# Cross-attention and routed FFN in one kernel: shared-weight splitting moved two row blocks ahead, two matmul chunks moved ahead of the last output products

## The chip, the cores and the metric

The kernel runs on one NeuronCore of one Trainium2 chip. The metric is the device time of one execution in microseconds. Before the change three runs took 1860.28, 1855.86 and 1855.59 us: median 1855.86 us.

## The reference

`x` has 4096 rows (4 x 1024) of 512 values. The block computes cross-attention against 64 keys per batch, and then a feed-forward network with one shared net and one of two routed experts:

```python
x = x + xattn(_layernorm(x), ctx, masks, Wq, Wk, Wv, Wo, bo)     # 16 heads of 64, softmax over 64 keys
z = _layernorm(x)
top1   = argmax(softmax(z @ gate_w.T))                            # one of 2 experts per row
expert = relu(z @ w1[top1] + b1[top1]) @ w2[top1] + b2[...]       # hidden size 2048
shared = relu(z @ sw1 + sb1) @ sw2 + sb2                          # hidden size 2048
x = x + expert + shared
```

## The kernel before

**Accuracy.** Operands of the large products are fp16 pairs, a high part and a low part, and each product is three matmuls (high x high, high x low, low x high). So the weights `sw1` and `sw2` of the shared net, which arrive as fp32, must be scaled and split into two fp16 halves before they can be used.

**Three stages.** Attention (until about 480 us) goes over 32 row blocks of 128 rows. The shared net goes over 16 tiles of 256 rows. The routed experts go over 17 tiles. All five engines run their own instruction streams, and semaphores tie them together. Between attention and the shared net TensorE has no barrier: it goes from the last `attend` straight to `shared_tensor`.

**A step of attention.** Every engine walks over steps t = N*g + u (N = 4), one for each row block, and in each step works on blocks at different distances: `step(eng, g, u, d, fn)` runs `fn` for block t + d. What an engine does in a step is in a fixed order:

- TensorE (`attend_tensor`): `t_p`(t) transposes the probabilities of block t into PSUM `pP` (L474, 8 matmuls); `sim`(t+2) makes the scores of block t+2 (L464, 24 matmuls of 512 columns); `attend`(t) makes the output product of block t (L485, 24 matmuls of 512 columns). `attend`(t) waits for `lo_p`(t). In steps 30 and 31 there is no `sim` left.
- ScalarE (`attend_scalar`): `hi_p`(t) (L540), `exp`(t+1) (L573), `scale_w`(t+2) (L567 and L569), `normal2`(t-1) (L554, L555), `normal`(t+4) (L546, L547).
- VectorE (`attend_vector`): `residual`(t-1) (L759), `lo_p`(t) (L703), sums, masks and statistics.
- GpSimd (`attend_gpsimd`): `lo_x`(t+3) (L344), two deviations, `norm`(t+1) (L659), `sub`(t+2) (L654), `low_w`(t+2) (L672), `lo_z`(t-1) (L668).
- SyncE (`attend_sync`) issues the DMAs of the step: `turn_x`(t+3), `load_x`, `load_m`, `load_r`(t+1), `store_x1`(t-2), `load_w`(t+3) (L393), `store_w`(t+1) (L401 and L402), `store_z`(t-2) (L416).

**Splitting of the shared weights.** Since `sw1` and `sw2` together are 32 pieces of 128 x 512, one piece is split in each step: `load_w` brings it into `sw`, `scale_w` writes the high half `swh` and scales `sw` in place, `low_w` writes the low half `swl`, `store_w` writes both halves to memory (`s1_split`, `s2_split`). All three buffers are double, by the piece's parity, and so every part waits for the piece two before it:

```python
def load_w(e, g, u):
    wait_apart(e, S["swl"], count(g, u) - 2)
def store_w(e, g, u):
    wait_apart(e, S["swl"], count(g, u))
def scale_w(e, g, u):
    e.wait_ge(S["sw_in", u % 2], dma_count2(g, u))
    e.wait_ge(S["sw_out", u % 2], 2 * dma_count2(g, u) - 32)
```

The last line is for both stores of piece r-2 to have landed before `scale_w`(r) writes `swh`. `count(g, u)` is the block's number plus one.

**Into the shared net.** The buffer `zT` of the shared net lies in the same room as `sw`, `swh` and `swl`, and the weight set `wA` in that of the folded attention weights, which `sim` reads. So `load_next` (SyncE, step 30) waits for all 32 pieces to be stored, issues two DMA transposes for `zT` (L1063), waits for `sim`(31), and loads the first quarter of the shared weights (`load_w1_w2(0)`: two DMAs at L1165, two at L1168, 512 KB each). The second quarter follows in step 32, the other two in `shared_sync`. Tile 0 of the shared net is 16 chunks: `first`(j) (L1081, 12 matmuls of 256 columns) makes 128 hidden columns, ScalarE and VectorE turn them into `hf`, `hh`, `hl`, and `second`(j) (L1093) follows two chunks later. `first`(j) waits for `hh` of chunk j-2.

## Time and profile before

| | before |
|---|---|
| time, median of 3 runs | 1855.86 us |
| profiled execution, its own time | 1857.37 us |
| span of the profiled execution | 1855.7 us |
| TensorE matmul busy | 1816.3 us (98%) |
| ScalarE busy | 820.8 us (44%) |
| VectorE busy | 797.8 us (43%) |
| GpSimd busy | 509.2 us (27%) |
| mean granted TensorE clock | 0.996 |

The profile is of one execution; its span runs from the first to the last instruction, and its own time is 1.7 us more. A busy share near 100% says that TensorE is the engine to look at, and then what counts is the few places where it stood still or ran slowly. In the rows further down, a row of a timeline gives the start in us, the length, the engine, the line, the operation with its output and input, and how many; in brackets stands how long the engine had been idle before and what released it. SPq is SyncE's queue of DMA issues, PEld the weight loads of TensorE.

### The profile page before, as it was taken

To read this page: it belongs to the slowest core of one execution; us is meant where nothing else is said; L and a number is where in the kernel's file an instruction comes from. 1 tells how busy PE (TensorE), PEld (TensorE's weight loads), DVE (VectorE), ACT (ScalarE), POOL (GpSimd) and SP (SyncE) were. 2 spreads that over 40 slices of the span, in tenths; PEclk is the share of its full clock that TensorE was granted. 3 is DMA by queue.
4 is the path that set the end of the run, shared out by engine and by line. 5 is a ranking of instruction groups with operands and counts; after the bars stand their busy time and mean duration, and the time that the engine had idled before them with its cause. 6 is when DMAs were issued, how large, how long until landed. Compare 5 with 4: busy or idle time off the path is not lost.

```text
span 1855.7 us, 33404 instructions
## 1 busy us (share of the span) xinstructions
PE 1816.3 (98%) x11516; PEld 1145.4 (62%) x11517; DVE 797.8 (43%) x1651; ACT 820.8 (44%) x1441; POOL 509.2 (27%) x475
## 2 busy tenths in 40 slices
PE   8989999999999999999999999999999999999997
PEld 6334444544566666666666666666666666666664
DVE  6987778777344333343433333222222222222222
ACT  4655555555333333334444444333333343333333
POOL 2047777777101111211100011312211221221210
PEclk9999999999999999999999999999999999999999
DMA  9246555655932332323444493921111122121100
GB/s 330 86 95 158 161 164 165 177 165 137 296 130 81 99 95 82 100 80 125 126 156 138 142 332 105 264 55 46 47 46 45 39 57 54 51 61 47 46 24 15
DMA packets 225955, 214.44 MB, mean 116 GB/s; under 512 B 126635, under 2 KB 168140, under 8 KB 225484
## 3 DMA queue, kind: packets, MB, share of 16 engines
q1 hardware_dynamic: 216924, 188.09, 34.4%
q0 software_dynamic: 8944, 25.19, 4.4%
q8 instruction: 54, 0.88, 0.2%
q14 instruction: 33, 0.27, 0.1%
HBM read 129.57 MB, written 59.02 MB: 102 GB/s over the span
## 4 chain that ended last, share of the span: by engine, by line
PE 88%; DVE 5%; POOL 2%; issue 2%; DMA 1%; ACT 1%; SPq 0%; POOLq 0%; DVEq 0%; ACTq 0%
PE pS L1081 36%; PE pP L1093 18%; PE pG L1093 9%; PE pO L1093 9%; PE pO L485 7%; PE banks_a L464 4%; PE pS L464 3%; DVE seen L799 2%; DVE room_w L819 1%; PE pP L474 1%; POOL room_b L659 1%; POOL room_b L654 1%; DMA e_split<-room_b 0%; POOL room_a L344 0%; PE banks_a L507 0%
## 5 line engine op out<-in xcount | busy, mean ns | idle before, releaser
L1081 PE MATMUL pS<-room_a,room_w 128*128 128x256 f16 (+1 forms) x6336 | 765.0, 271 | 1.5 <-issue 1.1
L1081 PEld LDWEIGHTS pS<-room_a,room_w 128*128 (+1 forms) x6336 | 611.2, 98 | 182.1 <-issue 10.2
L1112 DVE TENSOR_TENSOR room_a<-room_a 128x256 f16<-128x256 f32 (+1 forms) x528 | 237.6, 450 | 906.3 <-ACT room_a L1106 894.9
L1093 PE MATMUL pP<-room_w,room_a 128*128 (+1 forms) x1584 | 383.5, 379 | 0.1
L1104 ACT ACTIVATE room_a<-pS,room_b,sc 128x256 f32<-128x256 f32 (+1 forms) x272 | 151.7, 558 | 420.4 <-PE pS L1081 395.7
L1104 ACT ACTIVATE room_a<-pS,b1s,sc 128x256 f32<-128x256 f32 x256 | 144.2, 563 | 370.0 <-PE pS L1081 365.2
L1093 PEld LDWEIGHTS pP<-room_w,room_a 128*128 128x128 f16 x1584 | 154.8, 98 | 132.2 <-issue 0.7
L1093 PE MATMUL pG<-room_w,room_a 128*128 128x512 f16 (+1 forms) x768 | 207.6, 379 | 0.5 <-DVE room_a L1112 0.5
L1093 PE MATMUL pO<-room_w,room_a 128*128 128x512 f16 (+1 forms) x768 | 207.5, 379 | 0.0
L1128 POOL TENSOR_TENSOR room_a<-room_a,room_b 128x512 f32<-128x512 f32 x32 | 42.7, 1354 | 516.6 <-DVE room_a L1119 516.6
L485 PE MATMUL pO<-room_w,room_b 128*128 (+1 forms) x768 | 174.4, 384 | 7.6 <-DVE room_b L703 7.5
L1106 ACT ACTIVATE room_a<-pS,room_b,sc 128x256 f16<-128x256 f32 (+1 forms) x272 | 149.5, 550 | 0.0
L1106 ACT ACTIVATE room_a<-pS,b1s,sc 128x256 f16<-128x256 f32 x256 | 142.2, 556 | 0.0
L485 PEld LDWEIGHTS pO<-room_w,room_b 128*128 128x128 f16 x768 | 75.7, 99 | 101.3 <-DVE room_b L703 8.7
L1093 PEld LDWEIGHTS pO<-room_w,room_a 128*128 128x128 f16 x768 | 75.2, 98 | 90.6
L1508 POOL DMA_INDIRECT rows_room<-z_split,room_b x33 | 33.8, 1024 | 256.3 <-DVE room_b L1499 235.6
L1093 PEld LDWEIGHTS pG<-room_w,room_a 128*128 128x128 f16 x768 | 75.1, 98 | 40.6 <-DVE room_a L1112 0.8
L554 ACT ACTIVATE room_b<-room_b,shift,rs 128x512 f32<-128x512 f32 x32 | 26.1, 815 | 153.6 <-DVE shift L738 153.6
L464 PE MATMUL banks_a<-room_w,room_a 128*128 (+1 forms) x384 | 85.5, 379 | 3.2 <-DMA room_a<-room_a 1.6
L464 PE MATMUL pS<-room_w,room_a 128*128 (+1 forms) x384 | 85.5, 379 | 0.0
L1559 POOL DMA_INDIRECT out<-room_a,room_b x33 | 33.6, 1018 | 181.5 <-DVE room_a L1119 176.7
L1553 POOL TENSOR_TENSOR room_a<-room_a,room_b 128x512 f32<-128x512 f32 x33 | 44.0, 1350 | 113.8 <-DVE room_b L1641 113.8
(180 smaller groups left out, 1540.8 us busy)
## 6 DMA issues: line engine op xcount, KB each, us to landing
room_b<-in_w SPq DMA_DIRECT2D x64, 512.0 KB, 5.0
e_split<-room_b SPq DMA_DIRECT2D x64, 256.0 KB
room_w<-e_split SPq DMA_DIRECT2D x8, 2048.0 KB
rows_room<-in_x SPq DMA_DIRECT2D x32, 256.0 KB, 3.1
room_a<-in_sw SPq DMA_DIRECT2D x32, 256.0 KB, 4.2
room_b<-in_x SPq DMA_DIRECT2D x32, 256.0 KB, 3.8
s_split<-room_a SPq DMA_DIRECT2D x64, 128.0 KB, 3.7
x_scratch<-room_b SPq DMA_DIRECT2D x32, 256.0 KB, 4.0
```

The lines of the kernel that those rows point to most:

```text
L464: mm = e.matmul(pS[u % 2][:, h * 512:(h + 1) * 512], xT[:, u % 2, c, :], f[:, k, bass.ds(b, 1), h * 512:(h + 1) * 512], start=(n == 0), st ...
L485: mm = e.matmul(pO[:, :], pt[:, q, :], f[:, bass.ds(b, 1), q, :], start=(n == 0), stop=(n == 3 * PAIRS - 1))
L799: dve.tensor_reduce(dst, t, AX.X, ALU.max, apply_absolute_value=True).then_inc(done, 1)
L1081: mm = q.matmul(self.pH[j % 2][:, 0:rows], w[:, k, j * P:(j + 1) * P], zt[:, u, k, 0:rows], start=(n == 0), stop=(n == 3 * KC - 1))
L1093: mm = q.matmul(self.pY[u][r][:, :], h[:, j % self.HR, r * P:(r + 1) * P], w[:, j, :], start=(j == 0 and n == 0), stop=(j == HC - 1 and n ...
L1104: q.activation(self.hf[:, j % self.HR, 0:rows], self.pH[j % 2][:, 0:rows], ACT.Relu, bias=b, scale=self.a1)
L1106: q.activation(self.hh[:, j % self.HR, 0:rows], self.pH[j % 2][:, 0:rows], ACT.Relu, bias=b, scale=self.a1).then_inc(self.S["hh"], 1)
L1112: q.tensor_tensor(self.hl[:, j % self.HR, 0:rows], self.hf[:, j % self.HR, 0:rows], self.hh[:, j % self.HR, 0:rows], ALU.subtract).then_in ...
L1128: v = q.tensor_tensor(net.ob[:, u, r, :], net.ob[:, u, r, :], brow[:, :], ALU.add)
L1508: q.indirect_dma_start(dst[:, u, r, :], None, src, bass.IndirectOffsetOnAxis(ap=rows[:, u, r:r + 1], axis=0), bounds_check=ROWS - 1, oob_i ...
L1553: v = q.tensor_tensor(net.rb[:, u, r, :], net.rb[:, u, r, :], sel[:, u, :], ALU.add)
L1559: q.indirect_dma_start(out, bass.IndirectOffsetOnAxis(ap=io[:, u, r:r + 1], axis=0), net.ob[:, u, r, :], None, bounds_check=ROWS - 1, oob_ ...
```

## The change

`weight_steps(g, u, d)` gives the distances at which a part of the splitting runs in a step. In steps 0 to 3 it is d as before. In step 4 it is d and d+1, in step 5 it is d+1 and d+2, and from step 6 on it is d+2. So steps 4 and 5 handle two pieces each, and from then on every part works two pieces further ahead. SyncE, ScalarE and GpSimd use it for `load_w`, `store_w`, `scale_w` and `low_w`.

On SyncE `load_next`, now only the waits and the two transposes, moves from step 30 to step 28; the first quarter of the shared weights is loaded in step 29 and the second in step 30. On TensorE `first_chunk` puts chunks 0 and 1 of tile 0 between `t_p` and `attend` of steps 30 and 31, and `shared_tensor` leaves them out.

```diff
--- before.py
+++ after.py
@@ -339,6 +339,13 @@
 
                     return isinstance(g, int) and 0 <= N * g + u + d <= 1
 
+                def weight_steps(g, u, d):
+
+                    t = N * g + u if isinstance(g, int) else SUB
+                    if t < N:
+                        return (d,)
+                    return (d, d + 1) if t == N else (d + 1, d + 2) if t == N + 1 else (d + 2,)
+
                 def lo_x(e, g, u):
                     e.wait_ge(S["xn"], count(g, u))
                     e.tensor_tensor(xs[:, u % 2, DM:2 * DM], xnf[:, u % 2, :], xs[:, u % 2, 0:DM], ALU.subtract).then_inc(S["xl"], 1)
@@ -425,13 +432,19 @@
                                 sp.wait_ge(f_done, NF)
                             step(sp, g, u, 1, load_r)
                             step(sp, g, u, -2, store_x1)
-                            step(sp, g, u, 3, load_w)
-                            step(sp, g, u, 1, store_w)
+                            for d in weight_steps(g, u, 3):
+                                step(sp, g, u, d, load_w)
+                            for d in weight_steps(g, u, 1):
+                                step(sp, g, u, d, store_w)
                             step(sp, g, u, -2, store_z)
-                            if isinstance(g, int) and N * g + u == SUB - 2:
+                            if N * g + u == SUB - 4:
                                 load_next()
-                            if isinstance(g, int) and g == SUB // N and u == 0:
+                            if N * g + u == SUB - 3:
+                                sp.wait_ge(S["sim"], SUB)
+                                load_w1_w2(0)
+                            if N * g + u == SUB - 2:
                                 load_w1_w2(1)
+                            if g == SUB // N and u == 0:
                                 return
                     def load_next():
 
@@ -440,9 +453,6 @@
                             sp.wait_ge(S["z_out", u], 32)
                         for t in range(2):
                             snet.transpose(sp, t, z_d[t * TOK:(t + 1) * TOK, :])
-                        sp.wait_ge(S["sim"], SUB)
-                        load_w1_w2(0)
-
                     def load_w1_w2(q):
                         load_quarter(sp, wA, s1_d, s2_d, q, 1, first_in[f"w1_in{q}"])
                         load_quarter(sp, wA, s1_d, s2_d, q, 2, first_in[f"w2_in{q}"])
@@ -453,6 +463,12 @@
                     return last_block
 
                 def attend_tensor(pe):
+                    def first_chunk(e, j):
+                        if j == 0:
+                            e.wait_ge(S["smask"], SUB)
+                            e.wait_ge(first_in["w1_in0"], 32)
+                        snet.first(e, 0, 0, j, wA, 16)
+
                     def sim(e, g, u):
                         e.wait_ge(S["xT_in", u % 2], dma_count2(g, u))
                         at_least(e, S["smask"], count(g, u) - 2)
@@ -494,6 +510,8 @@
                             step(pe, g, u, 0, t_p)
                             if not first_tile(g, u, 0):
                                 step(pe, g, u, 2, sim)
+                            if isinstance(g, int) and SUB - 2 <= N * g + u < SUB:
+                                first_chunk(pe, N * g + u - SUB + 2)
                             step(pe, g, u, 0, attend)
 
                     pe.wait_ge(in_ctx, 16)
@@ -602,7 +620,8 @@
                             step(act, g, u, 0, hi_p)
                             step(act, g, u, 1, exp)
                             if not first_tile(g, u, 2):
-                                step(act, g, u, 2, scale_w)
+                                for d in weight_steps(g, u, 2):
+                                    step(act, g, u, d, scale_w)
                             step(act, g, u, -1, normal2)
                             if not early(g, u, 4):
                                 step(act, g, u, 4, normal)
@@ -693,7 +712,8 @@
                                 step(pool, g, u, 4, lo_x)
                             step(pool, g, u, 1, norm)
                             step(pool, g, u, 2, sub)
-                            step(pool, g, u, 2, low_w)
+                            for d in weight_steps(g, u, 2):
+                                step(pool, g, u, d, low_w)
                             step(pool, g, u, -1, lo_z)
                     groups(pool, SUB // N, body, peel_last=1)
 
@@ -1308,8 +1328,11 @@
 
     def shared_tensor(pe):
         def first(q, g, u, j):
-            if isinstance(g, int) and g == 0 and u == 0 and j % (HC // Q) == 0:
-                q.wait_ge(S[f"w1_in{j * Q // HC}"], 32)
+            if isinstance(g, int) and g == 0 and u == 0:
+                if j < 2:
+                    return
+                if j % (HC // Q) == 0:
+                    q.wait_ge(S[f"w1_in{j * Q // HC}"], 32)
             net.first(q, g, u, j, wA, 16)
 
         def second(q, g, u, j):
```

**SyncE in step 4, where the doubled steps begin.** A row is a line of the kernel, the operation with output and input, and in brackets the semaphores it waits for. `in_sw1` and `in_sw2` are the two weights; odd pieces are of `sw2`. Before, from `store_x1`(2):

```order
L412 DMA x1_scratch<-room_b 128x512 [waits a_x1]
L393 DMA room_a<-in_sw2 128x512 [waits a_swl]
L401 DMA s2_split<-room_a 128x512 [waits a_swl]
L402 DMA s2_split<-room_a 128x512
L416 DMA z_split<-room_b 128x1024 [waits a_z]
```

In the change:

```order
L419 DMA x1_scratch<-room_b 128x512 [waits a_x1]
L400 DMA room_a<-in_sw2 128x512 [waits a_swl]
L400 DMA room_a<-in_sw1 128x512 [waits a_swl]
L408 DMA s2_split<-room_a 128x512 [waits a_swl]
L409 DMA s2_split<-room_a 128x512
L408 DMA s1_split<-room_a 128x512 [waits a_swl]
L409 DMA s1_split<-room_a 128x512
L423 DMA z_split<-room_b 128x1024 [waits a_z]
```

The loads of pieces 7 and 8 now stand ahead of the stores of pieces 5 and 6, and those ahead of `store_z`(2). Step 5 has the same form with loads 9 and 10 and stores 7 and 8.

**ScalarE in step 4**, from `hi_p`(4) to `hi_p`(5). Before:

```order
L540 ACTIVATE room_b<-pP 128x1024 [waits a_att,a_pT]
L573 ACTIVATE room_b<-room_b 128x1024 [waits a_sub]
L567 ACTIVATE room_a<-room_a,sc 128x512 [waits a_sw_out0,a_swl,a_sw_in0]
L569 ACTIVATE room_a<-room_a,sc 128x512 [waits a_swh]
L554 ACTIVATE room_b<-room_b,shift2,rs2 128x512 [waits a_z_out1,a_rs2]
L555 ACTIVATE room_b<-room_b,shift2,rs2 128x512
L546 ACTIVATE room_a<-rows_room,shift1,rs1 128x512 [waits a_xT_in0,a_rs]
L547 ACTIVATE room_a<-rows_room,shift1,rs1 128x512
L540 ACTIVATE room_b<-pP 128x1024 [waits a_att,a_pT]
```

In the change:

```order
L558 ACTIVATE room_b<-pP 128x1024 [waits a_att,a_pT]
L591 ACTIVATE room_b<-room_b 128x1024 [waits a_sub]
L585 ACTIVATE room_a<-room_a,sc 128x512 [waits a_sw_out0,a_swl,a_sw_in0]
L587 ACTIVATE room_a<-room_a,sc 128x512 [waits a_swh]
L585 ACTIVATE room_a<-room_a,sc 128x512 [waits a_sw_out1,a_swl,a_sw_in1]
L587 ACTIVATE room_a<-room_a,sc 128x512 [waits a_swh]
L572 ACTIVATE room_b<-room_b,shift2,rs2 128x512 [waits a_z_out1,a_rs2]
L573 ACTIVATE room_b<-room_b,shift2,rs2 128x512
L564 ACTIVATE room_a<-rows_room,shift1,rs1 128x512 [waits a_xT_in0,a_rs]
L565 ACTIVATE room_a<-rows_room,shift1,rs1 128x512
L558 ACTIVATE room_b<-pP 128x1024 [waits a_att,a_pT]
```

`scale_w`(7), with its wait for the stores of piece 5 (`a_sw_out1`), now stands between `scale_w`(6) and `normal2`(3), and so ahead of `hi_p`(5).

**TensorE in steps 30 and 31.** Before:

```order
L474 MATMUL pP<-ident,room_b 128x128 x7
L485 MATMUL pO<-room_w,room_b 128x512 [waits a_x1,a_pTl]
L485 MATMUL pO<-room_w,room_b 128x512 x23
L474 MATMUL pP<-ident,room_b 128x128 [waits a_pTl,a_prob]
L474 MATMUL pP<-ident,room_b 128x128 x7
L485 MATMUL pO<-room_w,room_b 128x512 [waits a_x1,a_pTl]
L485 MATMUL pO<-room_w,room_b 128x512 x23
L1081 MATMUL pS<-room_a,room_w 128x256 [waits s_z_in0,s_w1_in0]
```

In the change:

```order
L490 MATMUL pP<-ident,room_b 128x128 x7
L1101 MATMUL pS<-room_a,room_w 128x256 [waits s_z_in0,s_w1_in0,a_smask]
L1101 MATMUL pS<-room_a,room_w 128x256 x11
L501 MATMUL pO<-room_w,room_b 128x512 [waits a_x1,a_pTl]
L501 MATMUL pO<-room_w,room_b 128x512 x23
L490 MATMUL pP<-ident,room_b 128x128 [waits a_pTl,a_prob]
L490 MATMUL pP<-ident,room_b 128x128 x7
L1101 MATMUL pS<-room_a,room_w 128x256 x12
L501 MATMUL pO<-room_w,room_b 128x512 [waits a_x1,a_pTl]
L501 MATMUL pO<-room_w,room_b 128x512 x23
L1101 MATMUL pS<-room_a,room_w 128x256 [waits s_hh]
```

The two chunks of 12 matmuls moved from behind the last output product into the places between transpose and product; the first one brings the wait for `zT` and the first quarter of `w1` with it.

## Rows read from the trace of the kernel before

**Rows 1.** The page: the chain that ended last, by engine

```profile
PE 88%; DVE 5%; POOL 2%; issue 2%; DMA 1%; ACT 1%; SPq 0%; POOLq 0%; DVEq 0%; ACTq 0%
```

**Rows 2.** Waits of TensorE over the whole span: in total, times, longest

```profile
PE pO L485 <- DVE room_b L703: 7.5, 4, 2.4
```

**Rows 3.** Timeline of the end of attention, steps 29 to 31, and tile 0

```profile
454.85 5.34 PE L485 MATMUL pO<-room_w,room_b 128*128 128x512 f16 x24
...
460.03 1.04 PE L474 MATMUL pP<-ident,room_b 128*128 128x128 f32 x8
...
462.16 1.22 DVE L703 SCALAR_TENSOR_TENSOR room_b<-pP,room_b 128x1024 f16<-128x1024 f32 x1 [0.45 <-ACT room_b L540]
...
463.44 7.04 PE L485 MATMUL pO<-room_w,room_b 128*128 128x512 f16 x24 [2.37 <-DVE room_b L703]
...
465.82 0.15 PEld L485 LDWEIGHTS pO<-room_w,room_b 128*128 128x128 f16 x1 [0.28 <-issue]
...
473.73 7.04 PE L485 MATMUL pO<-room_w,room_b 128*128 128x512 f16 x24 [2.37 <-DVE room_b L703]
...
480.61 4.09 PE L1081 MATMUL pS<-room_a,room_w 128*128 128x256 f16 x36
```

**Rows 4.** Busy time by stretch; the column after POOL is the granted TensorE clock

```profile
464.90:467.90 3.00, 3.00 (x8) 1.06 (x7) 1.28 (x6) 1.52 (x2) 2.66 (x3) 0.50 0.50 140
...
474.80:478.20 3.40, 3.40 (x9) 1.22 (x8) 1.20 (x7) 1.52 (x2) 1.15 (x1) 0.50 0.99 302
```

**Rows 5.** The chain that ended last, in order of time: one chunk

```profile
512.41 1.31 PE pS L1081 x12
```

**Rows 6.** Timeline of TensorE in step 0 of attention

```profile
118.39 5.35 PE L464 MATMUL banks_a<-room_w,room_a 128*128 128x512 f16 x24 [1.63 <-DMA room_a<-room_a]
...
127.00 5.35 PE L485 MATMUL pO<-room_w,room_b 128*128 128x512 f16 x24 [2.38 <-DVE room_b L703]
```

**Rows 7.** Timeline of steps 4 to 6

```profile
169.89 0.71 ACT L567 ACTIVATE room_a<-room_a,sc 128x512 f16<-128x512 f32 x1
...
170.63 0.72 ACT L569 ACTIVATE room_a<-room_a,sc 128x512 f32<-128x512 f32 x1
...
174.17 0.42 SPq L393 DMA_DIRECT2D room_a<-in_sw  x1
...
175.88 0.81 ACT L554 ACTIVATE room_b<-room_b,shift,rs 128x512 f32<-128x512 f32 x1 [4.53 <-DVE shift L738]
...
177.73 1.16 POOL L672 TENSOR_TENSOR room_a<-room_a 128x512 f16<-128x512 f32 x1
...
178.72 1.00 ACT L540 ACTIVATE room_b<-pP 128x1024 f16<-128x1024 f32 x1
...
182.43 1.21 DVE L703 SCALAR_TENSOR_TENSOR room_b<-pP,room_b 128x1024 f16<-128x1024 f32 x1
...
183.70 5.35 PE L485 MATMUL pO<-room_w,room_b 128*128 128x512 f16 x24 [0.36 <-DVE room_b L703]
...
190.98 1.16 POOL L672 TENSOR_TENSOR room_a<-room_a 128x512 f16<-128x512 f32 x1
...
195.32 5.34 PE L485 MATMUL pO<-room_w,room_b 128*128 128x512 f16 x24
```

**Rows 8.** The line L402, 160 to 450 us: its DMAs, from issue to landing

```profile
DMA to landing us min/median/max: 3.1/3.9/4.6
```

**Rows 9.** Timeline of SyncE's queue at the end of attention

```profile
445.27 0.54 SPq L401 DMA_DIRECT2D s_split<-room_a  x1
...
465.51 4.34 SPq L1063 DMA_TRANSPOSE room_a<-z_split  x2
...
470.19 0.93 SPq L1165 DMA_DIRECT2D room_w<-s_split  x2
```

**Rows 10.** DMAs issued at 470.0 to 471.1 us: size, us to landing

```profile
room_w<-s_split SPq DMA_DIRECT2D x2, 512.0 KB, 5.5
```

**Rows 11.** The line L1165 over the span: from issue to landing

```profile
DMA to landing us min/median/max: 5.0/8.0/9.0
```

## The prediction, made before the changed kernel was run

> **What bounds the kernel now.** I read the page's chain first, then who TensorE waited for, then the timeline at the two places that the change touches, then the granted clock there. The chain that ended last is TensorE for 88% [rows 1], so only its idle or slow stretches can be won, and every new one is lost in full. TensorE's costliest wait inside attention is that of `attend` for VectorE's `lo_p`: 7.5 us in four waits [rows 2]. Two of them, 2.37 us each, stand in steps 30 and 31. In a usual step `sim`(t+2) runs between `t_p` and `attend` and covers the way over `hi_p` and `lo_p`; in the last two steps nothing covers it. And after these two waits the 24 matmuls of `attend` take 7.04 us, where from 454.85 to 460.03 they took 5.18 [rows 3]. The weight loads show the pace there: 0.15 us and then 0.28 idle, 0.43 us a matmul [rows 3], and the granted clock is 0.50, the lower level of 1.2 GHz [rows 4]. So each of the two places holds 2.37 us of standstill and 7.04 - 5.18 = 1.86 us of slow clock.
>
> **The change at the end of attention.** Two chunks move from behind the last `attend` into these gaps. A chunk lasts 1.31 us at the full clock [rows 5]. It fits into 2.37 us, and `hi_p` and `lo_p` go on beside it unchanged, so 2 x 1.31 = **2.6 us** are won. What is left of each gap is 1.06 us. After 1.63 us of standstill in step 0 the next 24 matmuls took 5.35 us, and after 2.38 us also 5.35; the same idle of 2.37 us in steps 30 and 31 gave 7.04 [rows 3, 6]. So 2.4 us sometimes brings the lower clock and 1.6 us did not. I take it that 1.06 us does not, and book another 2 x 1.86 = **3.7 us**. Together **-6.3 us**; the bounds are -2.6 (clock falls all the same) and -6.3.
>
> The Trainium skill, "TensorE: Matmul & The Clock Gate", Part 1 (the HAM clock gate), says that the number of slow matmuls varies from run to run of one kernel, since the point where the clock changes does not follow the program. The trace agrees in that gaps of 2.37 and 2.38 us ended differently [rows 3, 6]. By that rule any value between the bounds is possible, and its price is the third rival below.
>
> Does the weight arrive in time? Chunk 0 can start when `t_p`(30) is done, at 463.44 - 2.37 = 461.07, and costs nothing up to 463.44 - 1.31 = 462.13 [rows 3]. SyncE stores the last piece in step 28, now 31 instead of 29, at about 445.3 to 445.9 [rows 9]; it lands 3.5 us later (the value is argued below), the two transposes take 4.34 us to issue [rows 9], and `load_r`, `store_x1` and `store_z` of step 29 some 1.4 us (three issues of 0.42 to 0.54 [rows 7, 9]): about 455. `sim`(31) ends at 454.85 [rows 3], so it does not hold it further. The two w1 loads are out by 455.9 (0.93 us for two [rows 9]), and landed 5.5 us after issue when the same load stood behind the same transposes [rows 10]: 461.0 to 461.4. That is in time, by less than 1 us. With 9.0 us to landing [rows 11] it would be 464.5. The stores of steps 28 to 30 and the second quarter have more room; chunk 2 needs `hh`(0) from chunk 0, and the whole `attend`(31), 5.18 us, lies between chunks 1 and 2 to cover it. After that the shared net runs as before.
>
> **The change in steps 4 and 5.** Here it adds waits. No work is added over the kernel, 32 pieces stay 32 pieces, but two are handled in each of these steps, and the order within SyncE and ScalarE makes a chain. `load_w`(8) waits for `low_w`(6), which GpSimd does late in step 4. Behind it on SyncE stand the stores of pieces 5 and 6 and `store_z`(2). `scale_w`(7) on ScalarE waits for the store of piece 5 to land. Behind `scale_w`(7) stand `normal2`(3), `normal`(8) and `hi_p`(5), and `hi_p`(5) releases `lo_p`(5), for which `attend`(5) waits. Worked out from the timeline of steps 4 to 6 [rows 7]:
>
> - `low_w`(6) ends at 177.73 + 1.16 = 178.9. Before, nothing on SyncE waited for it in that step: `load_w`(7) went out at 174.17 and the stores behind it.
> - The load and the high half go ahead of the low half, about 0.5 us each with what lies between: the low half is issued at 179.9.
> - Landing: 3.1 to 4.6 us, median 3.9, for this store [rows 8]. Those have up to a load, a transpose and two stores ahead; this one has one load and one store ahead and an otherwise empty queue. I take 3.5: 183.4.
> - `scale_w`(7) takes 1.46 us (169.89 to 171.35): 184.9.
> - `normal2` and `normal` take 178.72 - 175.88 = 2.84 us: `hi_p`(5) starts at 187.7 instead of 178.72.
> - `hi_p` 1.0, `lo_p` and release 463.44 - 462.16 = 1.3 [rows 3]: `attend`(5) starts at 190.0 instead of 183.70, **+6.3 us**.
>
> ScalarE's 4.53 us of idle before `normal2`(3) [rows 7] cannot hide it, since `scale_w`(7) would have to be done at 175.9 and gets its release at 183.4. Slack there is none: TensorE already waited 0.36 us for `lo_p`(5).
>
> Step 5 does it again: `load_w`(10) waits for `low_w`(8), the store of piece 7 stands behind it, `scale_w`(9) waits for that store, `hi_p`(6) stands behind `scale_w`(9). The place of `low_w`(8) in step 5 is that of `low_w`(7) before, whose end is 192.14 - 182.43 = 9.7 us after `lo_p`(5) began. The latter now begins at 188.7: `low_w`(8) ends at 198.4, the store has landed at 202.9, `hi_p`(6) starts at 207.2, `attend`(6) at 209.5 instead of 195.32: **+14.2 us** in all. From step 6 on each part again takes one piece, at the same distances between its partners as before; TensorE then has `sim` as cover and stands no more.
>
> TensorE stood idle some 6 us before each of these `attend`s, more than the 2.37 us that brought the lower clock twice. The slow stretch in `attend`(5) is hidden in the second standstill; that in `attend`(6) is not: **+1.9**, the price of rows 3. Early part: 14.2 + 1.9 = **+16.1 us**. Bounds: landing at 3.1 us in both chains and no slow clock gives 13.4, landing at 4.6 gives 18.3.
>
> The Trainium skill, "DMA: Bandwidth & Descriptors", section on latency and other measured facts, gives about 2 us as the fixed cost of a DMA. With 2.0 in place of 3.5 the estimate of the early part would be 3.0 less and the sum +6.8, 1862.7 us. No DMA of that line in the trace landed in under 3.1 us [rows 8], so I keep 3.5.
>
> **Sum.** +16.1 - 6.3 = **+9.8 us**. The profiled execution took 1857.37 us, so it would be 1867.2; that execution lies 1.5 above the median of the three runs. Against the median of 1855.86 the forecast is **1865.7 us**.
>
> **Rivals.**
> - *The doubled steps cost nothing.* The place is `scale_w`(7) in step 4. It costs nothing if its release comes by 175.88 - 1.46 = 174.4, into ScalarE's idle 4.53 us. Then only the gain is left: 1855.86 - 6.3 = 1849.5 us. For it: the total work is the same and ScalarE is 44% busy. Against it: in SyncE's order `load_w`(8) stands ahead of the store of piece 5, and it can't pass before 178.9. Chance 0.06.
> - *Only one of the two chains holds.* If in step 5 ScalarE's wait falls within a delay that step 4 has made for everybody, the early part is 6.3 + 1.9 = 8.2, the sum +1.9, 1857.8 us. For it: step 5 begins late on all engines. Against it: `low_w`(8) moves with `lo_p`(5), so the chain moves as a whole. Chance 0.13.
> - *The clock falls at the end all the same.* The gain is 2.6 and the sum 16.1 - 2.6 = +13.5: 1869.4 us. For it: TensorE is idle for 1.06 us behind a short chunk. Against it: 1.63 us did nothing in step 0. Chance 0.15.
> - *The first quarter comes late.* Landed at 464.5, chunk 0 ends at 465.8, 2.4 us after the old start of `attend`(30), and its clock stays low. Of the end are left +2.4 - 1.31 for chunk 0 and -1.31 - 1.86 for chunk 1, in sum -2.1: +14.0, 1869.9 us. This is also the case in which the change does not do what it says. For it: a margin under 1 us and loads of this line that took up to 9.0 us [rows 11]. Against it: 5.5 us for the comparable one [rows 10]. Chance 0.08.
>
> **How the numbers follow.** The forecast has 0.58. A measurement of this kernel can tell about 0.3%, 5.6 us, from no change. Forecast (its own bounds 1863.0 to 1868.0), third and fourth rival lie above 1861.4: slower 0.81. The second rival is the same, 0.13; the first is faster, 0.06. The range goes from 1857.5, which takes in the single chain, to 1871.5, the upper bound of the early part with the lower one of the gain (18.3 - 2.6 = +15.7).
>
> **What would show it.** In the changed profile, TensorE idle about 6 us before the `attend`s of steps 5 and 6, released by `lo_p`; ScalarE idle before the second `scale_w` of steps 4 and 5, released by a DMA `s_split<-room_a`; at the end one chunk of 12 matmuls in each gap, some 1 us idle behind it, and 5.2 instead of 7.04 us for the last two `attend`s. I am wrong if steps 5 and 6 start within 2 us of their old times, or if chunk 0 waits for a DMA.

## The result, and the profile after

The changed kernel took 1867.61 us (median of 6 runs, 1865.87 to 1871.35) against 1857.38 us for the kernel before (6 runs, 1855.59 to 1860.28): 10.2 us more, ratio 1.0059 with a 95% interval of 1.0045 to 1.0072. The forecast was +9.8 us. Of all executions timed below one is slow and stands in no ratio: one of the kernel with the unread matmuls, 2622.37 us at a mean granted clock of 0.685.

The page of the changed kernel: span, and the chain that ended last by engine.

```profile
span 1865.7 us, 33409 instructions
...
PE 91%; DVE 5%; DMA 1%; ACT 1%; issue 1%; POOL 1%; SPq 0%; ACTq 0%; POOLq 0%; DVEq 0%
```

The work is the same and TensorE still bounds the kernel, as in [rows 1]. What grew is its wait for `lo_p`, from 7.5 us [rows 2] to 14.2. Waits of TensorE, whole span: in total, times, longest.

```profile
PE pO L501 <- DVE room_b L723: 14.2, 4, 5.9
```

The timeline of the changed kernel in steps 4 to 7. The columns are those of [rows 7], which hold the same steps before; the first `attend` below is that of step 4.

```profile
175.62 5.34 PE L501 MATMUL pO<-room_w,room_b 128*128 128x512 f16 x24
...
180.38 1.16 POOL L691 TENSOR_TENSOR room_a<-room_a 128x512 f16<-128x512 f32 x1
...
182.42 0.43 SPq L409 DMA_DIRECT2D s_split<-room_a  x1
...
185.33 0.72 ACT L585 ACTIVATE room_a<-room_a,sc 128x512 f16<-128x512 f32 x1 [11.35 <-DMA s_split<-room_a]
...
186.71 0.80 ACT L572 ACTIVATE room_b<-room_b,shift,rs 128x512 f32<-128x512 f32 x1
186.72 0.75 DVE L779 SCALAR_TENSOR_TENSOR room_b<-pO,sc,room_b 128x512 f32<-128x512 f32 x1 [7.00 <-DMA z_split<-room_b]
...
189.53 1.00 ACT L558 ACTIVATE room_b<-pP 128x1024 f16<-128x1024 f32 x1
...
190.56 1.22 DVE L723 SCALAR_TENSOR_TENSOR room_b<-pP,room_b 128x1024 f16<-128x1024 f32 x1 [2.36 <-ACT room_b L558]
...
191.84 6.71 PE L501 MATMUL pO<-room_w,room_b 128*128 128x512 f16 x24 [4.82 <-DVE room_b L723]
...
199.12 1.16 POOL L691 TENSOR_TENSOR room_a<-room_a 128x512 f16<-128x512 f32 x1
...
201.15 0.43 SPq L409 DMA_DIRECT2D s_split<-room_a  x1
...
204.00 0.72 ACT L585 ACTIVATE room_a<-room_a,sc 128x512 f16<-128x512 f32 x1 [11.16 <-DMA s_split<-room_a]
...
210.52 7.61 PE L501 MATMUL pO<-room_w,room_b 128*128 128x512 f16 x24 [5.91 <-DVE room_b L723]
...
224.01 5.34 PE L501 MATMUL pO<-room_w,room_b 128*128 128x512 f16 x24
```

The reader is to follow one chain: `low_w`(6) ends at 181.54, SyncE issues the low half of piece 5 at 182.42, `scale_w`(7) starts when it has landed, after 11.35 us in which ScalarE did nothing, and everything down to `attend`(5) stands behind it. From 199.12 the same again. From the start of `attend`(4) to that of `attend`(7) are 48.39 us, before 206.55 - 171.94 = 34.61: **+13.8 us**.

The end of attention in the changed kernel, steps 29 to 31 and the first chunk of `shared_tensor` (compare [rows 3]):

```profile
471.15 5.34 PE L501 MATMUL pO<-room_w,room_b 128*128 128x512 f16 x24
...
478.33 1.47 PE L1101 MATMUL pS<-room_a,room_w 128*128 128x256 f16 x12 [0.97 <-issue]
479.74 5.35 PE L501 MATMUL pO<-room_w,room_b 128*128 128x512 f16 x24
...
485.81 1.47 PE L1101 MATMUL pS<-room_a,room_w 128*128 128x256 f16 x12
488.34 5.35 PE L501 MATMUL pO<-room_w,room_b 128*128 128x512 f16 x24 [1.07 <-DVE room_b L723]
493.53 1.47 PE L1101 MATMUL pS<-room_a,room_w 128*128 128x256 f16 x12
```

Both chunks run in the gaps and both `attend`s take 5.35 us. From `attend`(29) to chunk 2 are 22.38 us; before, chunk 2 came two chunks after 480.61, 483.22 - 454.85 = 28.37: **-6.0 us** in this pair of executions.

**The whole difference of the two spans, 10.0 us:** +3.7 before step 4 (`attend`(4) starts at 175.62 against 171.94), +13.8 in steps 4 to 6, -1.2 over steps 7 to 28 (247.14 against 248.30 us; 22 full steps of 11.23 are 247.1), -6.0 at the end, and -0.3 in the 1370 us that follow. The 1.2 us are small waits of the kernel before that are gone: five output products between steps 9 and 14 came 0.1 to 0.3 us late each, and TensorE's transposes waited four times for GpSimd's `norm` in steps 7 to 28; in the changed kernel each of these steps is 11.23 or 11.24 us long. The 3.7 us stand before anything that was changed. The first matmuls of the kernel before:

```profile
7.68 5.10 PE L507 MATMUL banks_a<-room_b,room_a 128*128 128x256 f32 x16 [7.68 <-DMA room_a<-in_wkT]
```

The same matmuls and the output product of step 0 of the changed kernel:

```profile
8.54 6.25 PE L525 MATMUL banks_a<-room_b,room_a 128*128 128x256 f32 x16 [8.54 <-DMA room_a<-in_wkT]
...
128.99 7.04 PE L501 MATMUL pO<-room_w,room_b 128*128 128x512 f16 x24 [2.38 <-DVE room_b L723]
```

The changed kernel began 0.9 us later behind an input DMA, its first 16 matmuls took 1.2 us longer, and the output product 1.7 us longer; before, the latter took 5.35 us behind the same idle [rows 6]. The product's slow matmuls stand at a lower granted clock (0.63 in the mean of 128.99 to 132.00 us). For the first 16 the profile shows a granted clock of 1.00 in both kernels, so that they were slower is shown, and why is not. So one pair of profiles can't settle a question of 3 us here, and the experiments below were timed in five rounds each.

### The profile page after: what moved, and what is told of

It is laid out like the page before. It is cut to its first block, busy times and chain, and to the rows that moved or that the text cites. A ratio compares the mean times of both kernels' runs of the same rounds, so it can differ in the third digit from the quotient of the medians.

```text
span 1865.7 us, 33409 instructions
## 1 busy us (share of the span) xinstructions
PE 1818.7 (97%) x11516; PEld 1146.8 (61%) x11517; DVE 797.3 (43%) x1651; ACT 822.5 (44%) x1441; POOL 510.3 (27%) x475
## 4 chain that ended last, share of the span: by engine, by line
PE 91%; DVE 5%; DMA 1%; ACT 1%; issue 1%; POOL 1%; SPq 0%; ACTq 0%; POOLq 0%; DVEq 0%
PE pS L1101 36%; PE pP L1113 18%; PE pG L1113 9%; PE pO L1113 9%; PE pO L501 9%; PE banks_a L480 4%; PE pS L480 4%; DVE seen L819 2%; DVE room_w L839 1%; PE pP L490 1%; PE banks_a L525 0%; DMA e_split<-room_b 0%; DMA room_a<-in_wkT 0%; PE banks_a L539 0%; DMA s_split<-room_a 0%
## 5 line engine op out<-in xcount | busy, mean ns | idle before, releaser
L501 PE MATMUL pO<-room_w,room_b 128*128 (+1 forms) x768 | 176.3, 387 | 14.2 <-DVE room_b L723 14.2
```

What stands on the lines that cost most here:

```text
L501: mm = e.matmul(pO[:, :], pt[:, q, :], f[:, bass.ds(b, 1), q, :], start=(n == 0), stop=(n == 3 * PAIRS - 1))
```

## The experiments

"Before" is the kernel before, run on the same chip between the others (medians 1857.1 to 1857.7 us). Timed kernels have 5 to 12 runs; they were timed in three groups on three chips (the first four versions below; early weights, one doubled step, w1 first and unread matmuls; transposes behind the stores and the changed kernel again), so versions of different groups are best compared by their distances to before; the spread of single runs of one kernel is about 2 us (standard deviation). Ratios are to before, with 95% intervals.

### The doubled steps alone

```diff
-                            if N * g + u == SUB - 4:
+                            if isinstance(g, int) and N * g + u == SUB - 2:
                                 load_next()
-                            if N * g + u == SUB - 3:
                                 sp.wait_ge(S["sim"], SUB)
                                 load_w1_w2(0)
...
-                                first_chunk(pe, N * g + u - SUB + 2)
```

> The changed kernel with its end of attention put back (second-step splitting stays doubled in steps 4 and 5, the first quarter of the weights is loaded in step 30, no chunk is moved). Theory (two chains over load_w, the store and scale_w in steps 4 and 5): the whole early cost without the gain, 14 to 16 us slower than before, about 1872 us, with TensorE idle 5 to 6 us before the output products of steps 5 and 6 and 7.0 us for each of the last two. Rival (the changed kernel is slow because its profiled execution lost 3.7 us before step 4 by chance, and the early part costs little): 4 to 8 us slower than before.

Measured: 1871.67 us, 14.2 above before, ratio 1.0074 (1.0061 to 1.0087). Its output products of steps 4 to 7:

```profile
174.12 5.34 PE L499 MATMUL pO<-room_w,room_b 128*128 128x512 f16 x24
...
190.19 8.01 PE L499 MATMUL pO<-room_w,room_b 128*128 128x512 f16 x24 [4.68 <-DVE room_b L719]
...
208.84 7.04 PE L499 MATMUL pO<-room_w,room_b 128*128 128x512 f16 x24 [4.58 <-DVE room_b L719]
...
221.77 5.34 PE L499 MATMUL pO<-room_w,room_b 128*128 128x512 f16 x24
```

The early cost is real, 14.2 us by the timed runs and 47.65 - 34.61 = 13.0 in this profile; the rival of a chance in the profiled pair falls. The idle times are 4.7 and 4.6 us, a little under the 5 to 6 expected. The products of steps 30 and 31 took 6.87 and 6.93 us behind 2.38 us of idle, as expected.

### SyncE's pairs taken apart

The changed kernel, with only SyncE's order in steps 4 and 5 different. `pair(k)` issues the load, then the store, of the k-th of the step's two pieces.

```diff
+                            two = len(weight_steps(g, u, 3)) == 2
+                            if two:
+                                pair(0)
                             step(sp, g, u, 3, turn_x)
...
-                            for d in weight_steps(g, u, 3):
-                                step(sp, g, u, d, load_w)
-                            for d in weight_steps(g, u, 1):
-                                step(sp, g, u, d, store_w)
+                            if not two:
+                                pair(0)
                             step(sp, g, u, -2, store_z)
+                            if two:
+                                pair(1)
```

> The changed kernel, with SyncE's two pairs of steps 4 and 5 taken apart: the first load and store stand at the head of the step, the second behind store_z. Theory: scale_w(7) and scale_w(9) find their stores landed before normal2 is ready, and the z stores no longer stand behind low_w, so the early cost falls from some 14 us to 0 to 2 and the gain of 6 us at the end stays: 4 to 6 us faster than before, 1851 to 1853 us. Rival (the cost comes from the doubled work on ScalarE and GpSimd itself, not from the order of SyncE's waits): as slow as the changed kernel, 8 to 10 us slower than before.

Measured: 1854.71 us, ratio 0.9983 (0.9975 to 0.9992): 2.7 us under before and 12.9 under the changed kernel. ScalarE's second `scale_w` of step 4:

```profile
174.07 0.72 ACT L592 ACTIVATE room_a<-room_a,sc 128x512 f16<-128x512 f32 x1 [0.48 <-DMA s_split<-room_a]
```

TensorE's output products of steps 4 to 6 in the same execution:

```profile
175.24 5.34 PE L508 MATMUL pO<-room_w,room_b 128*128 128x512 f16 x24
186.47 5.34 PE L508 MATMUL pO<-room_w,room_b 128*128 128x512 f16 x24
197.71 5.34 PE L508 MATMUL pO<-room_w,room_b 128*128 128x512 f16 x24
```

The doubled pieces cost ScalarE and GpSimd as much work as in the changed kernel, yet `scale_w`(7) waits 0.48 us instead of 11.35, and the output products follow each other every 11.23 us. It was the order of SyncE's waits, not the work. The gain, though, is 2.7 us and not the 4 to 6 expected.

### The pairs apart, with the old end

Both edits above together.

> The same order of SyncE, with the end of attention put back to that of before. Theory: within 2 us of before, 1856 to 1859 us, no wait of the output products of steps 5 and 6 over 1 us, the last two with 2.37 us of idle and 7.0 us each. Rival (doubled work costs by itself): 14 us slower than before.

Measured: 1858.42 us, ratio 1.0005 (0.9996 to 1.0013). In steps 5 to 29 no output product came more than 0.4 us late, and then:

```profile
464.47 5.35 PE L506 MATMUL pO<-room_w,room_b 128*128 128x512 f16 x24 [2.38 <-DVE room_b L726]
...
473.07 6.89 PE L506 MATMUL pO<-room_w,room_b 128*128 128x512 f16 x24 [2.38 <-DVE room_b L726]
```

So the lead of two pieces costs nothing when the pairs stand apart. The expectation of 7.0 us for both last products was wrong for one of them: the same idle of 2.38 us left the clock up once. The end is worth 1858.42 - 1854.71 = 3.7 us here, and 1871.67 - 1867.61 = 4.1 us between the doubled steps alone and the changed kernel.

### Load, store, load, store in the usual place

```diff
-                            for d in weight_steps(g, u, 3):
-                                step(sp, g, u, d, load_w)
-                            for d in weight_steps(g, u, 1):
-                                step(sp, g, u, d, store_w)
+                            for k in range(len(weight_steps(g, u, 3))):
+                                step(sp, g, u, weight_steps(g, u, 3)[k], load_w)
+                                step(sp, g, u, weight_steps(g, u, 1)[k], store_w)
```

> The changed kernel with load, store, load, store in the usual place of SyncE's steps 4 and 5, instead of two loads and then two stores. Theory: the store of piece 5 goes out before the wait for low_w(6), so scale_w(7) no longer holds; but store_z(2) and store_z(3) still stand behind low_w(6) and low_w(8), and residual and lo_p behind them on VectorE. The attends of steps 5 and 6 start 3.3 and 4.9 us later than in the step lengths of before, where the changed kernel showed 4.5 and 7.1; with slow clock after that the early part is about 10 us and the sum about 4 us slower than before, 1861 us. Rival (only the wait of scale_w for the stores counts): as fast as the version with the pairs taken apart, 4 to 6 us faster than before.

Measured: 1860.54 us, ratio 1.0016 (1.0008 to 1.0025), 3.1 us above before where 4 was expected. TensorE from step 4 to step 7:

```profile
173.91 5.34 PE L500 MATMUL pO<-room_w,room_b 128*128 128x512 f16 x24
187.47 7.04 PE L500 MATMUL pO<-room_w,room_b 128*128 128x512 f16 x24 [2.17 <-DVE room_b L722]
202.91 5.35 PE L500 MATMUL pO<-room_w,room_b 128*128 128x512 f16 x24 [2.34 <-DVE room_b L722]
214.54 5.34 PE L500 MATMUL pO<-room_w,room_b 128*128 128x512 f16 x24
```

ScalarE and VectorE in step 4 of the same execution, the second `scale_w`, `hi_p`(5), `residual`(4) and `lo_p`(5):

```profile
180.23 0.72 ACT L584 ACTIVATE room_a<-room_a,sc 128x512 f16<-128x512 f32 x1 [7.97 <-DMA s_split<-room_a]
...
184.43 1.00 ACT L557 ACTIVATE room_b<-pP 128x1024 f16<-128x1024 f32 x1
...
184.81 0.75 DVE L778 SCALAR_TENSOR_TENSOR room_b<-pO,sc,room_b 128x512 f32<-128x512 f32 x1 [6.59 <-DMA z_split<-room_b]
...
186.21 1.21 DVE L722 SCALAR_TENSOR_TENSOR room_b<-pP,room_b 128x1024 f16<-128x1024 f32 x1
```

The steps are 13.56 and 15.44 us long, before 11.76 and 11.62: 1.8 and 3.8 longer, where 3.3 and 4.9 were expected and the changed kernel has 4.5 and 7.1. So there are two holds in a doubled step. The wait of `scale_w` for its store is one. It is shorter here but not gone: 7.97 us of idle on ScalarE against 11.35. The z stores behind `low_w` are the other: `residual`(4) stood 6.59 us for one, and `lo_p`(5) began behind it, 0.8 us after `hi_p`(5) was done; in step 6 it was 2.1 us after. So here the z store's path ended last in both steps, and this order still costs 6.0 us up to `attend`(7), clock and all. In the changed kernel it is the other way round: `residual`(4) was done at 187.47, and `lo_p`(5) stood another 2.36 us for `hi_p`(5) (its row in the fence of the changed kernel), so the first hold hides the second. The rival (only `scale_w` counts) falls. How much each hold would cost alone no run shows.

### The weights early, but no chunk moved

The version with the pairs apart, without `first_chunk` and its `return` in `first`.

> The version with the pairs taken apart and the early load of the shared weights, but chunks 0 and 1 stay behind the last output product. Theory (the end gains only by filling the two standstills): as the version with the pairs apart and the old end, 1858 us, within 1.5 us of it; the two gaps of 2.4 us are there again. Rival (having the weights early helps by itself, since the loads no longer collide with the start of tile 0): 2 us or more faster than that, near the 1854.7 us with chunks.

Measured: 1860.34 us, ratio 1.0008 (0.9998 to 1.0017), 1.9 above the version with the pairs apart and the old end. The expected bound was 1.5; by the means it is 0.8, and the two intervals overlap. Both gaps of 2.37 us are there again, with products of 5.35 and 7.04 us behind them. What it tells apart is clear: it does not lie near the 1854.7 us with chunks, and loading the weights early showed no gain by itself. Against the version with the pairs apart only the place of the two chunks differs, and that is worth 5.6 us by the medians and 4.6 by the means (some 2 to 7 by the two intervals), of which 2.6 are the chunks.

### Only step 4 doubled

```diff
-                    return (d, d + 1) if t == N else (d + 1, d + 2) if t == N + 1 else (d + 2,)
+                    return (d, d + 1) if t == N else (d + 1,)
```

> Only step 4 is doubled (one piece ahead from step 5 on), SyncE in the changed kernel's order, the old end of attention. Theory (each doubled step is one chain of its own): one standstill of 4.5 us before the output product of step 5, then the lower clock in it for up to 1.7 us, so 5 to 6.5 us slower than before, 1862.5 to 1864 us, against 14.2 us for two doubled steps. Rival (the cost comes from two doubled steps in a row): under 2 us. Rival (the first doubled step makes nearly all of it): over 10 us.

Measured: 1865.12 us, ratio 1.0034 (1.0020 to 1.0047): 8.0 us above before by the medians, 6.6 by the means of its 5 runs and the 29 of before. That is above the 5 to 6.5 expected and under half of two steps' 14.2 only in the mean. Its profile is as expected, one hold of 4.67 us and a slow product:

```profile
174.77 5.34 PE L499 MATMUL pO<-room_w,room_b 128*128 128x512 f16 x24
190.83 6.77 PE L499 MATMUL pO<-room_w,room_b 128*128 128x512 f16 x24 [4.67 <-DVE room_b L719]
203.50 5.34 PE L499 MATMUL pO<-room_w,room_b 128*128 128x512 f16 x24
```

To `attend`(6) it is 28.73 us from `attend`(4), 5.35 more than before. So one doubled step holds by itself, and both rivals fall.

### w1 ahead of the transposes

The version with the pairs apart; the w1 half of the first quarter goes out in step 28, ahead of the transposes, and waits for the last score product of batch 2 instead of the last of all.

```diff
+                        sp.wait_ge(S["sim"], 3 * SUB // BATCH)
+                        load_quarter(sp, wA, s1_d, s2_d, 0, 1, first_in["w1_in0"])
                         for t in range(2):
                             snet.transpose(sp, t, z_d[t * TOK:(t + 1) * TOK, :])
...
                                 sp.wait_ge(S["sim"], SUB)
-                                load_w1_w2(0)
+                                load_quarter(sp, wA, s1_d, s2_d, 0, 2, first_in["w2_in0"])
```

> The version with the pairs apart; in addition the two w1 loads of the first quarter go ahead of the transposes in step 28, since their place in the room holds only folded weights of batches 0 and 2, so that they need not wait for the last score product. Theory: chunk 0 had waited 1 to 2 us for w1 and ran 0 to 0.9 us past the moment at which the output product could start; now it follows the transpose at once, the idle time lies behind it, and the time is 0 to 1 us below the 1854.7 us of the version without this. Rival (the transposes come later now and hold chunk 0): 1 us or more above it.

Measured: 1854.28 us, ratio 0.9984 (0.9975 to 0.9992); 0.4 us under the version without it, which the spread does not tell from nothing. TensorE in step 30 of this version:

```profile
460.35 1.04 PE L499 MATMUL pP<-ident,room_b 128*128 128x128 f32 x8
461.22 1.47 PE L1110 MATMUL pS<-room_a,room_w 128*128 128x256 f16 x12
464.58 5.35 PE L510 MATMUL pO<-room_w,room_b 128*128 128x512 f16 x24 [1.89 <-DVE room_b L732]
```

SyncE's queue in the same execution:

```profile
450.45 6.68 SPq L1092 DMA_TRANSPOSE room_a<-z_split  x2
...
458.28 0.43 SPq L423 DMA_DIRECT2D z_split<-room_b  x1
```

Chunk 0 no longer waits (1.95 us in the profile of the version with the pairs apart, 0.97 in that of the changed kernel). But the idle behind it is 1.89 us, not 1.06: the transposes held SyncE for 6.68 us, `store_z`(27) went out at 458.28, and `residual`(29) waited 2.84 us for it, ahead of `lo_p`(30).

### The transposes behind the stores

```diff
                             if N * g + u == SUB - 3:
+                                turn_z(0)
                                 sp.wait_ge(S["sim"], SUB)
...
                             if N * g + u == SUB - 2:
+                                turn_z(1)
                                 load_w1_w2(1)
```

This is the version with w1 first; `turn_z` is one transpose each, and they leave `load_next`.

> The version with pairs apart and w1 first; the transpose for tile 0 moves behind the stores of step 29 and the one for tile 1 to step 30. Theory: in the version before, the two transposes held SyncE for 6.7 us and so store_z(27), on which residual(29) and lo_p(30) waited, which put the output product of step 30 off by 0.8 us. Now chunk 0 follows t_p at once and the output product starts 3.4 us after t_p, with 1.06 us of idle: 0.5 to 1 us below the 1854.3 us of that version, about 1853.5 us. Rival (the transpose for tile 0 now comes too late for chunk 0): no gain or 1 us slower.

Measured: 1854.18 us, ratio 0.9979 (0.9969 to 0.9988), 3.5 us under before. Step 30:

```profile
461.67 1.04 PE L503 MATMUL pP<-ident,room_b 128*128 128x128 f32 x8
...
465.09 5.35 PE L514 MATMUL pO<-room_w,room_b 128*128 128x512 f16 x24 [1.06 <-DVE room_b L736]
```

The order works as expected, 3.42 us from `t_p` to `attend` and 1.06 idle. The time does not show the 0.8 us: 0.1 less by the medians; but the two versions were timed on different chips, and against before it is 3.5 us here and 2.8 there, 0.7 less. The spread tells neither from nothing. By its median this is the fastest form that was run, faster than both kernels, but the three forms with the pairs apart can't be ranked among each other.

### Matmuls that nobody reads, in the kernel before

```diff
+                            if isinstance(g, int) and SUB - 2 <= N * g + u < SUB:
+                                filler(pe)
                             step(pe, g, u, 0, attend)
```

The 12 matmuls in each of steps 30 and 31 are added work whose result is dropped.

> The kernel before, with 12 matmuls of 256 columns that nobody reads put in each of the two gaps before the last two output products. They take the place of idle time only, so what changes is TensorE's clock. Theory (1.06 us of idle does not bring the lower clock, 2.37 us does in most but not all executions): the last two output products take 5.35 us each in the profile, and the median falls by 1 to 3.4 us, 1854 to 1856.5 us. Rival (the lower clock comes at 1.06 us too, or hardly ever came at 2.37): no change within 0.5 us, and the gain at the end is the chunks' 2.6 us alone.

Measured: 1857.41 us, ratio 0.9998 (0.9989 to 1.0007): no change, against the expected fall of 1 to 3.4 us. Its profile shows both products at 5.35 us, as the theory had it:

```profile
465.82 5.35 PE L491 MATMUL pO<-room_w,room_b 128*128 128x512 f16 x24 [1.06 <-DVE room_b L711]
...
474.42 5.35 PE L491 MATMUL pO<-room_w,room_b 128*128 128x512 f16 x24 [1.06 <-DVE room_b L711]
...
480.23 4.10 PE L1089 MATMUL pS<-room_a,room_w 128*128 128x256 f16 x36 [0.46 <-DMA room_w<-s_split]
```

Tile 0 now starts before the first quarter has landed and waits for it, 0.9 us in two waits, which takes back part. In its number this is what the rival expected, and its reason (that the lower clock comes at 1.06 us too, or hardly ever at 2.37) does not fit the profiles, which are counted below; what the clock at these two places is worth in the average execution stays open. The interval reaches from -2.0 to +1.3 us, so with the 0.9 added back an average worth of the clock of up to some 2.9 us is not excluded; a regular gain of 3.4 is.

### The changed kernel again

> The changed kernel once more, to set its steps beside those of the others on one chip: 1867 to 1868 us. In its profile TensorE stands 4.5 to 6 us before the output products of steps 5 and 6 as in the first one. What differs from execution to execution is the start (5.1 to 6.5 us for the first 16 matmuls) and whether the output product of step 0 takes 5.35 or 7.04 us behind 2.38 us of idle.

Measured: 1868.03 us, ratio 1.0056 (1.0043 to 1.0069). The output products of steps 5 and 6:

```profile
190.93 6.78 PE L501 MATMUL pO<-room_w,room_b 128*128 128x512 f16 x24 [4.80 <-DVE room_b L723]
...
209.55 7.70 PE L501 MATMUL pO<-room_w,room_b 128*128 128x512 f16 x24 [5.79 <-DVE room_b L723]
```

From `attend`(4) at 174.73 to `attend`(7) at 223.14 are 48.41 us, as in the first profile (48.39). The chain repeats to within 0.1 us; chunk 0 waited 1.55 us this time and not 0.97.

## Why the prediction was right

**The sum** of +9.8 us met a measured +10.2. Both of its terms were too large, by about 2 us each, and this cancelled: the direction and the place are earned, that the sum is met within 0.4 us is luck. The forecast time, 1865.7 us, lies 1.9 under the 1867.61 measured; 1.5 of that is that it counts from 1855.86 us, the median of the first three runs of before, where that of all six is 1857.38.

**Steps 4 and 5** were forecast at +16.1 us. The profile shows 13.8, and the kernel with the doubled steps alone 14.2 by its runs and 13.0 in its profile. The chain is the one that the prediction wrote down, waiter by waiter. What was off are sizes:
- `attend`(5) was put 6.3 us late; it came 4.5 us late, counted from `attend`(4) (16.22 against 11.76). The landing of the store was taken as 3.5 us and was 185.33 - 182.42 = 2.9, under the 3.1 that [rows 8] give as the least of 160 to 450 us (over the whole trace of before it is 3.0), and `low_w`(6) ended 5.9 us after the start of `attend`(4), not 7.0.
- The second chain was forecast at 19.5 us from `attend`(5) to `attend`(6) and took 18.7. `low_w`(8) ended 9.7 us after `lo_p`(5) began, as worked out; its store landed after 2.85 us.
- The slow clock behind the second hold was put at +1.9 and was 13.49 - 11.23 = 2.3. That in `attend`(5) was hidden, as forecast: `attend`(6) waited for `lo_p` long after `sim`(8) was done.
- One hold was missing from the account. `store_z`(2) was named as standing behind `load_w`(8), but not that `residual`(4), and with it `lo_p`(5), waits for it. In the changed kernel this is hidden, in the order load, store, load, store it ended last.
- The fixed cost of about 2 us from the Trainium skill ("DMA: Bandwidth & Descriptors", latency and other measured facts) would have given 1862.7 us; with 2.9 us per store the truth lay between it and the 3.5 taken, and the sum lay with the latter only because the other term was off too.

**The end** was forecast at -6.3 us. The pair of profiles shows -6.0. The pairs of timed kernels show -4.1 and -3.7. The step that failed is the clock's term, booked as 2 x 1.86 with certainty. Its size was 1.69, not 1.86: the 7.04 us of a row must be set against the 5.35 of the same row elsewhere, and not against the 5.18 from one start to the next. And it isn't paid in every execution. In the profiles of before, of the doubled steps alone, of the pairs apart with the old end, of the early weights without chunks and of the single doubled step, the idle of 2.37 us stands ten times, and the product behind it took 6.87 to 7.04 us seven times and 5.35 three times. The profile of before, on which the term rests, showed it both times. By place it is five of five in step 31 and two of five in step 30. The remark that 2.4 us only sometimes brings the lower clock was in the prediction; it should have gone into the sum as a share. With 0.7 x 1.69 for each the end comes to 2.6 + 2.4 = 5.0 us, and with chunk 0 up to 0.9 us late to 4.1. That the filled gap keeps the clock up held in all profiles: 1.06 us of idle was followed by 5.35 us nine times out of nine. The filler in the kernel before did not confirm the average worth; how much the clock gives there stays open between nothing and some 2.9 us by that run; the version without moved chunks points at 2 to 3 us, with nothing still inside its interval.

**The rivals.** That the doubled steps cost nothing fell with the doubled steps alone. That only one of the two chains holds fell with the two holds in every profile of the changed order. That the clock falls at the end all the same was not seen. The late first quarter came about by half: chunk 0 did wait for a DMA, 0.97 and 1.55 us in the two profiles of the changed kernel, which the prediction had named as a sign of being wrong (the trace gives no releaser for chunk 0; in the first profile the later of its two w1 loads, issued at 471.8, landed 6.5 us later, and the chunk began at 478.33). So w1 came 0.6 and 1.2 us after the latest time forecast, 461.4 in the times of before, and this cost nothing in the one profile and under half a us in the other.

**Where it could be mended.** The gain did not need the loss. With SyncE's pairs apart the same lead costs nothing: 1854.71 and 1854.18 us.

## What to carry to other kernels

When a pipeline step is doubled to get ahead, write down for each in-order queue what stands behind the doubled instructions: with two buffers the second one waits for a full round trip (compute, store, landing) of the piece before, and here that put 11 us of idle on ScalarE and held work that had nothing to do with it. Look at every waiter of every entry behind the pair: here the z store behind it was a second path to the same product. Put the issue of the pair at the points of the queue where its waits are already met, one at the head and one at the end of the step.

A term that rests on the clock after a short idle is to be booked with the share in which several profiles show it, not with its full size from one.

## What was not expected of the hardware

Behind 2.37 or 2.38 us of idle in a stretch otherwise busy, the next 24 matmuls took 5.35 us or 6.85 to 7.04, and which of them changed from execution to execution at the same place of the program: it was the slow one in step 0 in ten of twelve profiles (not in before and not in the version with w1 first) and in step 30 in two of five. In step 31 it was the slow one in all five. It isn't the length of the idle alone either: with load, store, load, store 2.17 us was followed by 7.04 us and 2.34 us by 5.35, and with w1 first 1.89 us by 5.35. Behind 4.6 to 5.9 us of idle it was 6.7 to 8.0 us each time. The first 16 matmuls of the kernel took 5.10 to 6.5 us. Added up, 1.4 us at the start and 1.7 in each of steps 0 and 30 come to some 4.8 us, and 6.5 if step 31 can be fast too (an estimate from these rows), where the runs of before spread over 7.1 us (1854.8 to 1861.9). That the one makes the other is not shown: of before only one execution was profiled.

The two DMA transposes, issued one behind the other, took 4.1 to 6.7 us of SyncE's queue (4.34 before [rows 9]), and issued apart 5.04 and 2.99 us; what sets the length no run shows. What stands behind them waits that much longer.
